# Self-attention of 16-wide heads: queries masked to four heads of 64 rows instead of eight of 128

## The reference

```python
def split(x, w, bb):                     # 16 heads of 16 dims
    return (x @ w + bb).reshape(B, -1, H, hd).transpose(0, 2, 1, 3)
...
q = split(q_in, qw, qb) * hd ** (-0.5)
k = split(k_in, kw, kb)
v = split(v_in, vw, vb)
s = jnp.einsum('bhqd,bhkd->bhqk', q, k)
if mask is not None:
    s = jnp.where(mask, -jnp.inf, s)
a = jax.nn.softmax(s, axis=-1)
o = jnp.einsum('bhqk,bhkd->bhqd', a, v)
...
x = features + _mha(xn, xn, xn, ..., causal)   # xn: layer norm of the block's input
```

## Time and profile before

| | |
|---|---|
| median of three runs | 1972.47 us (1972.38 to 1973.41) |
| the profiled execution: its time, its span | 1972.66 us, 1970.9 us |
| busy share of the span | PE 88%, PEld 63%, DVE 66%, ACT 43%, POOL 36% |
| the chain that ended last, by engine | PE 41%, DVE 20%, issue 18%, POOL 14% |
| mean granted TensorE clock | 0.967 of full speed |
| L0_sa in the span | from some 20 to 135 us |
| L1_sa in the span | from some 593 to 715 us |

### The profile page before, as it was taken

How to read it: one execution, slowest core, us unless ns; L and a number is a source line. 1 busy time by engine, 2 the same in 40 slices (tenths; PEclk the granted TensorE clock), 3 DMA queues, 4 the chain that set the end, 5 groups by cost and what they waited for, 6 DMA issues and landing times.

```text
span 1970.9 us, 35184 instructions
## 1 busy us (share of the span) xinstructions
PE 1742.6 (88%) x11106; PEld 1235.4 (63%) x11106; DVE 1298.0 (66%) x3310; ACT 843.0 (43%) x2473; POOL 705.1 (36%) x796
## 2 busy tenths in 40 slices
PE   5979998889997888988799999898888989999998
PEld 4756665679975667555674444585445955555567
DVE  5866677511137876888775565896778966666675
ACT  3645554333335643666324443342232445445431
POOL 2325555220022234676423332340001435555443
PEclk9989999789998989999999999999999989999999
DMA  4100000388961001102100020101001000000200
GB/s 173 37 23 13 16 8 16 108 293 323 322 230 69 0 1 32 33 31 74 70 9 17 16 72 0 54 1 65 0 0 61 16 1 13 23 11 11 75 1 19
DMA packets 37006, 115.13 MB, mean 58 GB/s; under 512 B 3345, under 2 KB 23729, under 8 KB 29729
## 3 DMA queue, kind: packets, MB, share of 16 engines
q1 hardware_dynamic: 34352, 107.33, 15.7%
q0 software_dynamic: 2544, 6.43, 1.0%
HBM read 99.34 MB, written 14.40 MB: 58 GB/s over the span
## 4 chain that ended last, share of the span: by engine, by line
PE 41%; DVE 20%; issue 18%; POOL 14%; ACT 4%; DMA 2%; DVEq 0%; POOLq 0%; SPq 0%; ACTq 0%
POOL arena L2102 10%; PE ps L1057 6%; PE ps L1097 5%; PE ps L1207 4%; PE ps L1219 4%; PE ps L862 3%; PE ps L990 2%; PE ps L857 2%; PE ps L968 2%; DVE arena L1784 2%; PE ps L842 2%; ACT arena L1340 2%; PE ps L902 1%; PE ps L935 1%; PE ps L835 1%
## 5 line engine op out<-in xcount | busy, mean ns | idle before, releaser
L2102 POOL TENSOR_TENSOR arena<-arena,rinv 112x375 f32<-112x375 f32 (+1 forms) x448 | 370.6, 829 | 470.4 <-DVE rinv L1767 459.7
L935 PEld LDWEIGHTS ps<-cst,arena 112*125 112x125 f32 (+1 forms) x1408 | 183.8, 180 | 167.7 <-POOL arena L2102 81.9
L935 PE MATMUL ps<-cst,arena 112*125 112x112 f32 (+1 forms) x1408 | 242.6, 289 | 39.6 <-POOL arena L2102 36.5
L1340 ACT ACTIVATE arena<-ps,negmax 112x375 f32<-112x375 f32 (+1 forms) x384 | 190.3, 501 | 159.2 <-DVE negmax L1762 158.8
L1776 DVE COPY arena<-ps 125x336 f32<-125x336 f32 x384 | 190.4, 496 | 39.3 <-PE ps L935 37.8
L1762 DVE TENSOR_REDUCE negmax<-ps 112x1 f32<-112x375 f32 (+1 forms) x288 | 158.1, 549 | 69.2 <-PE ps L907 61.9
L1340 ACT ACTIVATE arena<-arena,negmax 112x112 f32<-112x112 f32 (+1 forms) x256 | 125.5, 491 | 138.9 <-DVE negmax L1751 93.0
L1057 PE MATMUL ps<-h_split_sb,w_split_sb 128*128 128x448 f32 x768 | 171.9, 371 | 7.7 <-DVE h_split_sb L1620 3.0
L1057 PEld LDWEIGHTS ps<-h_split_sb,w_split_sb 128*128 128x128 f32 x768 | 145.0, 190 | 23.8 <-POOL w_split_sb L2178 4.9
L857 PE MATMUL ps<-wat,arena 128*125 128x256 f32 (+1 forms) x576 | 145.3, 388 | 8.9 <-ACT arena L1279 7.5
L990 PE MATMUL ps<-wat,arena 128*112 128x256 f32 x512 | 126.5, 392 | 9.4 <-DVE arena L1786 3.7
(11 more groups left out here) (230 smaller groups left out, 3262.6 us busy)
## 6 DMA issues: line engine op xcount, KB each, us to landing
wml<-in_wm_L_moe SPq DMA_DIRECT2D x21, 1028.0 KB, 7.2
wml<-in_wm_L_moe SPq DMA_DIRECT2D x21, 1024.0 KB, 8.2
craw<-in_ctx SPq DMA_DIRECT2D x32, 375.0 KB
wml<-in_wm_L_m SPq DMA_DIRECT2D x3, 3072.0 KB, 13.8
wat<-in_wa_L_ca SPq DMA_DIRECT2D x2, 2560.0 KB, 9.6
wml<-in_wm_L_m SPq DMA_DIRECT2D x2, 2048.0 KB, 9.9
keys_hbm<-arena SPq DMA_DIRECT2D x8, 375.0 KB
arena<-keys_hbm SPq DMA_DIRECT2D x8, 375.0 KB
```

Of the source, the lines that this page charges most:

```text
L935: last = nc.tensor.transpose(ps[0:blk.kp, T_BANK + s % blk.t_banks, o:o + S], buf[:, i * blk.nk + q * blk.kp:i * blk.nk + (q + 1) * blk.kp ...
L1340: last = go(probs[0:S, s % blk.nprobs, i * nk:(i + 1) * nk], src[:, i * nk:(i + 1) * nk], ACT.Exp, scale=-1.0 if blk.mask == "input" else ...
L2102: pool.tensor_tensor(p3, p3, r3, ALU.mult).then_inc(scaled, 1)
```

## The change

Q and K leave their projection in another order of columns: the host permutes the columns of the two weights and biases (`halves`), so that the four heads of a unit lie in 64 consecutive rows, unit s in chunk s // 2 and half s % 2. The spread then needs four copies per chunk instead of eight: copy i keeps head i of the upper half and head i of the lower half. `scores` reads only the 64 rows of its unit, as weights and as moving data. The list `HALVES`, which would make units of two steps go together, is empty, so n is 1 and the units go one by one, in the same places as before.

```diff
--- before.py
+++ after.py
@@ -103,6 +103,7 @@
 
 
 AHEAD = "L1_ca"
+HALVES = ()
 PAIRS = ("L0_ca", "L1_ca", "L2_ca", "L2_sa", "L3_ca")
 KEY_SCALE = ("L2_sa",)
 
@@ -129,6 +130,7 @@
         self.no = 1 if dh == 16 else 2
         self.wg = 1 if dh == 16 else 2
         self.pairs = name in PAIRS
+        self.halves = name in HALVES
         self.ahead = name == AHEAD
         plan = SCHEDULES[name]
         self.plan, self.dve, self.pool = plan["plan"], plan["dve"], plan["pool"]
@@ -882,7 +884,7 @@
 
                 def scores(b, s):
 
-                    n = 2 if blk.pairs else 1
+                    n = 2 if blk.pairs or blk.halves else 1
                     free = masked if blk.mask == "causal" else maxed if blk.mask else exped
                     base = st["masked"] if blk.mask == "causal" else st["turn"] if blk.mask else st["unit"]
                     wait(pe, free, count(base, units, b, s + n - blk.s_banks))
@@ -917,12 +919,13 @@
                         mm(ps[0:blk.kp, blk.bank_at(s), 0:HG * S], kT[:, parity(b), g // 2, q * blk.kp:(q + 1) * blk.kp],
                            qz[:, parity(b), HG * g:HG * (g + 1)], start=True, stop=True).then_inc(scored, 1)
                         return
-                    for i in range(blk.heads):
-                        u = s * blk.heads + i
-                        last = mm(ps[0:S, blk.bank_at(s), i * blk.nk:(i + 1) * blk.nk],
-                                  qz[:, parity(b), head_of(u) if blk.dh == 16 else u],
-                                  kT[:, parity(b), u // 8, 0:blk.nk], start=True, stop=True)
-                    last.then_inc(scored, 1)
+                    for i in range(HG):
+                        for z in range(n):
+                            c, rows = (s + z) // 2, slice(64 * ((s + z) % 2), 64 * ((s + z) % 2) + 64)
+                            last = mm(ps[0:S, blk.bank_at(s + z), i * S:(i + 1) * S], qz[rows, parity(b), 4 * c + i],
+                                      kT[rows, parity(b), c, 0:S], start=True, stop=True)
+                            if i == HG - 1:
+                                last.then_inc(scored, 1)
 
                 def turn(b, s):
 
@@ -1009,7 +1012,7 @@
                     for s in steps(b, blk, blk.out_step + 1):
                         if b == B and s in warm.get("tail", {}):
                             keep_busy(spare, warm["tail"][s])
-                        if b != B and (s % 2 == 0 or not blk.pairs):
+                        if b != B and (s % 2 == 0 or not blk.pairs and not blk.halves):
                             scores(b, s)
                         at = lagged(b, s, lag, units)
                         if at and not blk.keys_first:
@@ -1664,10 +1667,10 @@
                     elif name == "spread":
 
                         dve.wait_ge(w_full, count(st["w"], np_, m, blk.pieces.index("Q") + 1))
-                        m16 = cs("mask16", 8).unsqueeze(2).broadcast_to([P, 8, S])
+                        m16 = cs("mask16of64", 4).unsqueeze(2).broadcast_to([P, 4, S])
                         for c in range(DC):
                             W = ps[:, blk.w_banks[blk.bank_of["Q"]], c * S:(c + 1) * S]
-                            last = v.scalar_tensor_tensor(qz[:, par, 8 * c:8 * c + 8], W.unsqueeze(1).broadcast_to([P, 8, S]),
+                            last = v.scalar_tensor_tensor(qz[:, par, 4 * c:4 * c + 4], W.unsqueeze(1).broadcast_to([P, 4, S]),
                                                           cs(blk.name + "_bq", DC)[:, c:c + 1], m16, ALU.add, ALU.mult)
                         last.then_inc(w_done[blk.bank_of["Q"]], 1)
                     elif name == "qsq":
@@ -2219,6 +2222,7 @@
 
     order = np.concatenate([np.arange(64) + 64 * h for c in range(8) for h in (8 * (c // 4) + c % 4, 8 * (c // 4) + 4 + c % 4)])
 
+    halves = np.array([16 * (8 * c + 2 * i + z) + d for c in range(DC) for z in range(2) for i in range(4) for d in range(16)])
     vec = {
         "L0_sa_g": a[L0 + "sa_ln_g"], "L0_sa_b": a[L0 + "sa_ln_b"],
         "L0_ca_g": a[L0 + "ca_q_ln_g"], "L0_ca_b": a[L0 + "ca_q_ln_b"],
@@ -2235,6 +2239,9 @@
         for i, x in enumerate("qkv"):
             vec[f"{blk}_b{x}"] = a[f"{L0}{pre}_in_b"][i * D:(i + 1) * D]
             vec[f"L1_{pre}_b{x}"] = a[f"{L1}{pre}_{x}b"]
+            if pre == "sa" and x in "qk":
+                for name in (f"{blk}_b{x}", f"L1_{pre}_b{x}"):
+                    vec[name] = vec[name][halves]
 
     consts = np.zeros((P, NCOL), np.float32)
 
@@ -2278,8 +2285,9 @@
 
     for pre in ("sa", "ca"):
         w = a[f"{L0}{pre}_in_w"]
-        attn("L0_" + pre, w[:D].T, w[D:2 * D].T, w[2 * D:].T, a[f"{L0}{pre}_out_w"].T)
-        attn("L1_" + pre, *(a[f"{L1}{pre}_{x}w"] for x in "qkvp"))
+        heads = halves if pre == "sa" else np.arange(D)
+        attn("L0_" + pre, w[:D].T[:, heads], w[D:2 * D].T[:, heads], w[2 * D:].T, a[f"{L0}{pre}_out_w"].T)
+        attn("L1_" + pre, a[f"{L1}{pre}_qw"][:, heads], a[f"{L1}{pre}_kw"][:, heads], a[f"{L1}{pre}_vw"], a[f"{L1}{pre}_pw"])
     for pre, s in (("ca", "c"), ("sa", "s")):
         attn("L2_" + pre, a[f"{L2}wq_{s}"].reshape(D, -1)[:, order], a[f"{L2}wk_{s}"].reshape(D, -1),
              a[f"{L2}wv_{s}"].reshape(D, -1), a[f"{L2}wo_{s}"][order])
```

## The result

| | before | after |
|---|---|---|
| median of 12 runs each, beside one another | 1972.54 us (1968.64 to 1976.87) | 2000.28 us (1982.99 to 2007.54) |
| ratio, 95% interval | | 1.0125 (1.010 to 1.0151): slower |
| the profiled execution: time, span | 1972.66, 1970.9 us | 2001.2, 1999.4 us |
| its mean granted clock | 0.967 | 0.951 |

The forecast was 1975.9 us, 1972.4 to 1980.0. The change cost 28 us where 3.4 were counted.

A forecast was written before the change was run, and what follows sets the result against it. No engine is full; the ring of waits between batches bounds the blocks, through PE in L0_sa. L0_sa +3.2 and L1_sa +0.2 make +3.4 us, for 1975.9 us, range 1972.4 to 1980.0.

The forecast's parts named there:

- The step that failed: Scores in both blocks: same number of matmuls and loads, same columns, so a unit stays at 0.95 us.
- the 0.09 that the prediction adds for the first load: Going into a 64-row unit of scores, its first weight load lies in the open: 0.09 us.
- The granted clock falls in these blocks: Rival, chance 0.05: units take 1.8 times as long at 1.2 GHz in both self blocks; total 1980 to 2016 us.
- if the clock differs in the two blocks: One of the signs in L0_sa and L1_sa by which the prediction would count itself wrong; no size given.
- The steps for L0_sa: L0_sa: height switches lengthen PE's chain, 0.44 per period; with the block's ends, +3.2 us.
- the spread pair: Two DVE spread instructions per batch, halved in length: 1.2 to 1.3 us instead of 2.21, 0.95 saved.
- L1_sa's steps at 2.4 GHz: L1_sa batches: gains before the update and losses at later scores nearly cancel, mean +0.05, +0.3 us for six batches.
- the 0.95 counted: Start of L1_sa: the shorter spread stands in a gapless row of DVE instructions, so 0.95 us is saved.
- The 0.87 for the batch behind it: L1_sa's following batch, at 1.2 GHz: switches at 1.8 times the price, +0.87 us.
- The switch is free here: Rival, chance 0.07: 64-row scores follow full-height work without emptying the array; L0_sa gains nothing, L1_sa gains; 1968.8 us.
- A load can't overlap a matmul in the same half: Rival, chance 0.03: a unit's loads and matmuls run one behind the other, +0.79 us a unit; about 1998 us.

The follow-up runs named there:

- pairs: The changed kernel with the score units of two steps issued together in both blocks, one in each half of the array: 1991.19 us, ratio 1.0089.
- second profile: The changed kernel run and profiled again with nothing altered: 1997.22 us, ratio 1.0111 to the kernel before.
- small spread, full rows: The changed kernel with its four-copy spread, but scores multiplying all 128 rows: 1971.21 us, ratio 0.999 to the kernel before.
- half rows, the same added matmul: The changed kernel with one 16-column matmul on the unit's own 64 rows added ahead of every unit of scores: 2019.97 us, ratio 1.0215.
- half-height fillers: The changed kernel with four 64-column matmuls on the unit's own 64 rows added ahead of every unit of scores: 2020.30 us, ratio 1.0252.

## Why the prediction was wrong, point by point

**The step that failed** is a term that the sum doesn't have: new time at the lower clock. "Their streaming time goes by columns (112 before and after), so I leave a unit at its 0.95" prices the scores at 2.4 GHz, and only the one batch of L1_sa that had been low before is priced lower. At 2.4 GHz the step is right (a unit takes 1.03, with the 0.09 that the prediction adds for the first load); but the height of the scores also bears on which clock is granted. What the runs showed in its place: 18.97 for a batch that takes 10.68 at 2.4 GHz, 28 us in all, and the clock and the time of before when the scores alone go back to 128 rows (1971.21 us). The sum puts such falls at nothing. The rival "The granted clock falls in these blocks" had the right event and place and a range that holds the result (1980 to 2016), gave no cause, and got 0.05. It was put aside for one row: 64-row scores at 2.4 GHz from 146 to 166. That row is from L0_ca, with 375 columns per matmul and both halves issued in turn; with the 112-column scores of the self blocks, pairs did not hold the clock either. The prediction's own sign of being wrong, "if the clock differs in the two blocks", is the one that came.

**The steps for L0_sa came right.** Period 11.95 for 11.9, Q to U 4.94 for 4.9, the spread pair 1.28 for 1.26 (2.21 less 0.95). In the second profile, where L0_sa kept its clock up to 121 us, it runs from its first Q (21.44) to its last update (126.01) in 104.57; before it was 123.21 − 22.17 = 101.04. That is 3.5 more; the sum had 3.2.

**L1_sa's steps at 2.4 GHz came close.** From 646 to 693 in the first profile its updates are 12.83, 12.99 and 12.83 apart (from 648.44 to 687.09), where before they were 12.6 and 13.0 in turn: some +0.1 per batch, where the sum had +0.05. DVE waits for the scores at three of the mask additions of a batch, where the prediction counted two, those of steps 3 and 0. The third, of step 2, waited 0.21 before the change (at 649.97) and waits 0.40 now (timeline of DVE, the last bracket is the wait):

```profile
650.26 0.62 DVE L1762 TENSOR_TENSOR arena<-ps,cst 112x448 f32<-112x448 f32 x1 [0.25 <-PE ps L925]
...
654.96 0.62 DVE L1762 TENSOR_TENSOR arena<-ps,cst 112x448 f32<-112x448 f32 x1 [0.40 <-PE ps L925]
...
659.36 0.62 DVE L1762 TENSOR_TENSOR arena<-ps,cst 112x448 f32<-112x448 f32 x1 [0.58 <-PE ps L925]
```

At the head of the block the pair of spreads starts at 611.70 and takes 1.27:

```profile
611.70 1.27 DVE L1673 SCALAR_TENSOR_TENSOR arena<-ps,cst 128x448 f32<-128x448 f32 x2 [2.08 <-PE ps L837]
...
615.77 0.63 DVE L1762 TENSOR_TENSOR arena<-ps,cst 112x448 f32<-112x448 f32 x1
```

From its start to the first mask addition there are 4.07, against 5.00 before: 0.93 gained of the 0.95 counted. The 0.87 for the batch behind it can't be read by itself, since the clock was low there for longer than before (618.4 to 625.2 and 632.0 to 645.7; before 606.3 to 609.7 and 616.6 to 626.8).

**The other rivals.** "The switch is free here" falls: the scores' load starts at 71.41, 0.31 after V's last matmul (71.10), and the next period is longer as counted. "A load can't overlap a matmul in the same half" falls: eight loads in one half take 0.86 within the 1.03 of their matmuls. With the sentence of the Trainium skill's page "TensorE: Matmul & The Clock Gate", section "The mechanism", that a load overlaps matmuls in flight only when their row groups differ, these rows disagree as those before the change did.

**Shown and not shown.** Shown: the loss goes when the scores alone go back to 128 rows; the changes of height, with the scores on 128 rows, leave the clock; with equal instructions, 64 rows lose it. The zeros in the copies don't decide it: 16 filled rows per copy kept the clock in 128 rows and lost it in 64, and 32 filled rows in 128 (small spread, full rows) kept it. Not shown: why 64 rows count for less; how much other work makes up for them, since L0_sa with 64-row scores also kept 2.4 GHz for 95.6 us on end in the second profile; and what decides between a fall at the head of L0_sa and falls through L1_sa. The untouched block (matmuls 6900 to 7200) loses 2.6 us in both profiles to a low stretch of 6.8 us that the kernel before doesn't have (1058.7 to 1065.5 in the first). The small spread with full rows has one of 3.4 us in the same block (1030.5 to 1033.9), so this part needs no 64-row scores; what brings it on is open.

## What to carry to other kernels

Making matmuls less high saves PE no time when their columns stay, and can cost the clock of a block: price such a change at both levels of the clock, and give the lower one a real chance, even in a block that kept the higher one before. PE's busy share alone is no evidence either way; here 0.82 held 2.4 GHz with 128 rows and 0.93 did not with 64. That a stretch of other work keeps its clock, with other columns, in another order, says little about the work at hand, and one profile shows one outcome of several: look at the clocks of all runs.

## What the runs showed of the hardware

With 128-row scores the clock held at 0.82 busy (L1_sa before, 626.8 to 715.6). With 64-row scores it fell after a stretch at 0.93 (half rows, the same added matmul, 657.4 to 674.5) and held at 0.99 (half-height fillers, 662.8 to 748.2). In the changed kernel's first profile 23.90 us at 1.2 GHz passed, all of them busy, before it returned. The Trainium skill, "TensorE: Matmul & The Clock Gate", section "What's actually happening", says that the clock is set by how busy PE has been; these runs differ from it if busy means PE's time alone.

What was also not expected is how much of the run-to-run spread one such block makes: the kernel before ran within 8 us, the changed one within 25, and over its 18 runs in the two series the time follows the mean clock almost alone.
